# First layer of a graph network: 18 scatters and 8 dense tiles, then 17 and 9, in place of 18 and 8 in both halves of a loop body

## The reference, cut to what matters

```python
def scatter_mean(src, index, dim_size):
    s = jax.ops.segment_sum(src, index, num_segments=dim_size)
    cnt = jax.ops.segment_sum(jnp.ones((src.shape[0],), src.dtype), index, num_segments=dim_size)
    return s / jnp.maximum(cnt, 1.0)[:, None]

edge_attr_agg = scatter_mean(edge_attr, edge_index[0], x.shape[0])
combined = jnp.concatenate([x, edge_attr_agg], axis=1)
h = jax.nn.relu(combined @ W1 + b1)
return h @ W2 + b2
```

## Time and profile before

| | |
|---|---|
| median of 3 runs | 7578.14 us (7569.88 to 7579.32) |
| the profiled execution | 7575.93 us |
| its span, first to last instruction | 7574.1 us |
| VectorE busy, share of the span | 6223.6 us, 82% |
| GpSimd busy, share of the span | 5347.8 us, 71% |
| granted TensorE clock, mean | 0.835 |

### The profile page before, as it was taken

One profiled execution on the slowest core, in us unless ns is written; L12 is line 12 of the kernel. 1 busy time (PEld: TensorE's weight loads), 2 busy tenths in 40 slices (PEclk: granted clock), 3 DMA queues, 4 the chain that ended last, 5 costly groups with the idle time before them and its releaser, 6 DMA issues. The chain is left out here.

```text
span 7574.1 us, 145887 instructions
## 1 busy us (share of the span) xinstructions
PE 6258.4 (83%) x38830; PEld 4411.6 (58%) x38831; DVE 6223.6 (82%) x16834; ACT 4861.8 (64%) x11241; POOL 5347.8 (71%) x4893
## 2 busy tenths in 40 slices
PE   6988888888867999975777777777777999999995
PEld 3545545544546888865666666666674544444443
DVE  7999999999969999957999999999986555555554
ACT  5777778778737888844555555555524677777773
POOL 4888888888865566657777777777513777777776
PEclk9999999999978999965666666666655999999997
DMA  5444444444431111124343444444331222222222
GB/s 130 75 75 72 69 75 72 69 75 72 66 74 39 24 24 24 24 53 63 64 65 64 64 65 64 65 64 65 55 93 47 65 76 70 70 70 76 70 70 55
DMA packets 626461, 487.11 MB, mean 64 GB/s; under 512 B 513289, under 2 KB 530030, under 8 KB 616344
## 3 DMA queue, kind: packets, MB, share of 16 engines
q0 software_dynamic: 281600, 185.95, 21.1%
q1 hardware_dynamic: 342455, 293.43, 13.3%
q10 hardware_dynamic: 2304, 6.55, 0.3%
HBM read 303.43 MB, written 182.13 MB: 64 GB/s over the span
## 5 line engine op out<-in xcount | busy, mean ns | idle before, releaser
L977 POOL DMA_INDIRECT acc<-val,idx x1116 | 1722.6, 1544 | 379.5 <-issue 320.4
L1601 POOL DMA_INDIRECT tile_rows<-att_row_table,src_by_tile x1620 | 1531.0, 945 | 502.9 <-issue 490.9
L748 PE MATMUL banks<-part 128*128 128x490 bf16 (+1 forms) x7440 | 1569.5, 366 | 218.8 <-DVE part L831 218.8
L3032 POOL DMA_INDIRECT rows_l<-relation_table,idx x1302 | 1245.7, 957 | 430.6 <-issue 386.4
L3237 PE MATMUL banks<-h_parts,dense_onehot 128*128 128x448 bf16 x6510 | 1316.2, 359 | 102.2 <-ACT dense_onehot L2985 99.7
L2270 PE MATMUL banks<-tile_rows,prob 128*128 x4032 | 854.1, 380 | 539.8 <-DVE kept_l L2368 538.7
L748 PEld LDWEIGHTS banks<-part 128*128 128x128 bf16 x7440 | 694.3, 97 | 996.7 <-DVE part L831 280.9
L2270 PEld LDWEIGHTS banks<-tile_rows,prob 128*128 128x128 f32 x4032 | 769.0, 285 | 638.0 <-issue 637.9
L3237 PEld LDWEIGHTS banks<-h_parts,dense_onehot 128*128 128x128 bf16 x6510 | 620.5, 99 | 730.0 <-issue 178.7
L907 ACT ACTIVATE digit_distance<-iota_row,dst_digits_negated 128x128 bf16<-128x128 f32 (+1 forms) x3224 | 868.7, 357 | 2.1 <-ACT dst_digits_negated L896 0.2
L1296 POOL DMA_INDIRECT gathered_rows<-h_table,gathered_index x600 | 579.4, 966 | 397.3 <-DMA gathered_rows<-h_table,gathered_index 245.7
(11 more groups left out here) (449 smaller groups left out, 11835.1 us busy)
## 6 DMA issues: line engine op xcount, KB each, us to landing
src_rows<-src_by_column SPq DMA_DIRECT2D x63, 1152.0 KB, 5.9
piece_sums<-kept_l SPq DMA_DIRECT2D x252, 264.0 KB
running_sums<-run SPq DMA_DIRECT2D x62, 832.0 KB, 4.1
attr<-in_edge_attr SPq DMA_DIRECT2D x61, 624.0 KB
tile_rows<-att_row_table,src_by_tile POOLq DMA_INDIRECT x1620
rows_l<-relation_table,idx POOLq DMA_INDIRECT x1302
dense_code_rows<-src_by_column SPq DMA_DIRECT2D x62, 320.0 KB
acc<-val,idx POOLq DMA_INDIRECT x1116
```

Source lines behind the costliest of these rows:

```text
L748: last = e.matmul(ps[a][:, 0:ZW[a]], place0[(h * NZ + m) % 2][:, a, :], spread0[(h * NZ + m) % 2][n].rearrange("p b f -> p (b f)")[:, 0:ZW ...
L977: e.indirect_dma_start(acc_d[k], bass.IndirectOffsetOnAxis(ap=idx[h][:, r:r + 1], axis=0), val[h][:, r, :], None, compute_op=ALU.add).then ...
L1601: e.indirect_dma_start(to, None, hx_d, bass.IndirectOffsetOnAxis(ap=src_col[:, t:t + 1], axis=0))\
L3032: e.indirect_dma_start(g[h][:, r, :], None, y3_d, bass.IndirectOffsetOnAxis(ap=idx[h][:, r:r + 1], axis=0))\
```

## The change

In the second half of a loop body one tile goes dense instead of by scatter: 17 scatters in groups of 4, 4, 4, 4 and 1, and 9 dense tiles (spreads 4 to 8 one behind the other). The first half keeps 18 and 8. HS and NZ become pairs. The tile counters of dense tiles run over 17 tiles a loop (`z_count`). As 17 is odd, the buffer of a dense tile is now its number in its half, modulo 2: the last tile of a second half (m = 8) and the first one of the next first half (m = 0) then take the same buffer, and that first spread waits for one `z_add` more. The accumulator of a scatter is its number in the loop body, modulo 4; with 35 scatters in a loop the first three of the next one follow the last one into the same accumulator after three steps instead of four. Ahead of the loop, two of VectorE's instructions that split source numbers into digits become two each, and the scratch for the digits shares the room of `place0`.

```diff
-HS = 18
-NZ = HALF - HS
+HS = (18, 17)
+NZ = (HALF - HS[0], HALF - HS[1])
+NZL = NZ[0] + NZ[1]
+NSL = HS[0] + HS[1]
...
-        GROUPS = [(r, min(r + 4, HS)) for r in range(0, HS, 4)]
+        GROUPS = [[(r, min(r + 4, HS[h])) for r in range(0, HS[h], 4)] for h in range(2)]
+        ADDS = [len(range(k, NSL, NACC)) for k in range(NACC)]
...
+            hots0 = borrow(0, ZA * P)
+            place0 = [hots0.bitcast(bf16)[:, k * ZA * P:(k + 1) * ZA * P].rearrange("p (a c) -> p a c", c=P) for k in range(2)]
...
+            def z_count(i, h):
+                return i * NZL + h * NZ[0]
...
                             def z_add(m):
-                                e.wait_ge(s_spread, hh * NZ + m + 2)
+                                e.wait_ge(s_spread, z_count(i, h) + m + 2)
...
-                            for m in range(NG - 1, NZ):
+                            for m in range(NG - 1, NZ[h]):
                                 z_add(m)
...
-                    e.tensor_scalar(dig_i, src_z, 21400.0, None, ALU.mult).then_inc(s_digits, 1)
+                    e.tensor_scalar(of_half(dig_i, 0), src_z[0], 21400.0, None, ALU.mult)
+                    e.tensor_scalar(of_half(dig_i, 1), src_z[1], 21400.0, None, ALU.mult).then_inc(s_digits, 1)
...
                     def rest_one(hh, h):
...
-                        e.tensor_tensor(left0[0], pack[h][:, HS:HALF, :], high0[0], ALU.subtract).then_inc(s_left, 1)
+                        e.tensor_tensor(left0[0][:, 0:NZ[h], :], pack[h][:, HS[h]:HALF, :], high0[0][:, 0:NZ[h], :],
+                                        ALU.subtract).then_inc(s_left, 1)
...
                     def spread(hh, h, m):
...
-                        e.wait_ge(s_z, hh * NZ + m + 1)
-                        b = (h * NZ + m) % 2
+                        e.wait_ge(s_z, z_count(i, h) + m + (2 if m == 0 and h == 0 else 1))
+                        b = m % 2
...
-                            for k, (lo, hi) in enumerate(GROUPS):
+                            for k, (lo, hi) in enumerate(GROUPS[h]):
...
-                            for m in range(NG - 1, NZ):
+                            for m in range(NG - 1, NZ[h]):
                                 spread(hh, h, m)
...
-                            for r in range(HS):
-                                q, k = divmod(h * HS + r, NACC)
-
-                                e.wait_ge(s_add[k], (i * (2 * HS // NACC) + q) * 16 + 16)
+                            for r in range(HS[h]):
+                                q, k = divmod(h * HS[0] + r, NACC)
+
+                                e.wait_ge(s_add[k], (i * ADDS[k] + q) * 16 + 16)
```

## The result

The changed kernel takes 7659.49 us (median of 5 runs, 7657.05 to 7663.82) against 7572.81 us for the kernel before, measured beside it: a ratio of 1.0113, 95% interval 1.0098 to 1.0128. It is slower, by 87 us. The profiled execution took 7663.82 us, 87.9 us more than that of before. The prediction said 7654 us. All ratios in this document leave out the one execution that took far longer than the others, 18358 us, in the run of the kernel before with short target rows.

A forecast was written before the change was run, and what follows sets the result against it. The prediction took GpSimd (66.50 us a loop) to bound the kernel, VectorE with TensorE close behind: 65.56 + 2.78 + 0.58 = 68.92 us a loop, ending 78 us later. 7575.93 + 78 = 7654 us, range 7595 to 7680 us.

The forecast's parts named there:

- Two cycles: Late loop before the change: GpSimd's 66.50 us sets the pace, VectorE with TensorE needs 65.56 us, a slack of 0.94 us.
- The rule on occupancy: Highest occupancy marks the bottleneck: VectorE, 62.3 of 66.5 us, so the change would cost about 74 us; the prediction rejected it.
- The ninth tile: Spread 8, end of a second half: costs TensorE's step, 3.05 us a loop, bounds 2.65 to 3.05 us.
- The missing scatter tile: VectorE, second half: one compare of 0.27 us and 0.13 us of the `eq` compare saved, -0.40 us.
- The new wait: Spread 0 of a first half waits for `z_add` 8: 0.58 us on VectorE, bounds nothing to 3.05 us.
- Landings at three steps: GpSimd, first three scatters of a loop: taken as nothing, at most 4.6 us; slower rival 7700 us, chance 0.05.
- The base and what grew: VectorE's loop before the change, 65.56 us; `rest_one` and `rest_two` grow by 0.07 us each, 0.13 us for both.
- The sum: VectorE's loop becomes 68.92 us, last spread ends at 2206.8 us, whole kernel 7654 us; chance 0.73.
- The little-change rival: VectorE's loop: waits shrink, 67.12 us a loop, 7599 us, chance 0.11; within 15 us of no change, 0.04.

## Why the prediction was right, point by point

*Two cycles.* GpSimd was the pace of the kernel before: the shorter target rows gained nothing there, and its scatters fell behind the target rows until ACT's wait held the rest. VectorE with TensorE stood 1 us behind it: taking 7.4 us from GpSimd gained 1.1 us a body (65.4 for 66.5). That the slack was 0.94 us and not VectorE's 4.2 us of idle time decided the sign, and it was read off the first halves, in which GpSimd wasn't yet behind.

*The rule on occupancy* (the Trainium skill, page "Perfetto Trace Analysis", section "Identifying the Most-Contended Engine"). It named VectorE, by 94%, as what bounds the kernel before. The run with short target rows there (0.9996) contradicts it; in the changed kernel, where VectorE is busy 64.6 of 68.8 us, the same edit is worth 39 us of loop.

*The ninth tile* cost TensorE's step, 3.05 us (1030.60 to 1033.65), as taken; removing its wait gave back 0.33 us a body.

*The missing scatter tile* saves 0.48 us by the run with 18 and 9, not 0.40. A compare of 128 columns for `eq` takes 0.29 us in the changed kernel, as the slope gave; the other 0.08 us lies in and around the target rows.

*The new wait* measured 0.62 us of idle time for a forecast of 0.58, and in the kernel before it cost nothing, since it lay within the slack.

*Landings at three steps* were taken as nothing, and the run with 14 scatters shows that they were. Their upper bound of 4.6 us was far off: exposed, they reached 1.5 us at the longest and 1.8 us a body (57.0 / 31), of which 0.9 us is more than issue. The 1.3 us a loop of landing waits that the prediction adds beside them stands in no row: 26.2 us in 31 bodies are 0.85, and 65 x 0.3 us of them would be issue anyway.

*The base and what grew.* The 65.56 us read from the first six halves were 0.23 too long (65.33 with 14 scatters). `rest_one` and `rest_two` grew by 0.05 us each (0.62 for 0.57, 0.61 for 0.56), 0.10 for 0.13. And the target rows take 1.95 us a body in the changed kernel against 1.73 with 14 scatters in the kernel before (means); the sum has no term for these 0.22 us (next section). Put together, 65.33 + 3.05 - 0.48 + 0.10 + 0.62 + 0.22 = 68.84 us, which is what the trace shows. The base and the missing term cancel, and that is luck.

*The sum:* a body of 68.83 us against 68.92, and a start at 103.05 instead of 103.63 us, make the loop some 3.5 us shorter than forecast (30 x 0.09, 0.58 at the start, 0.22 in the first second half), which would have ended it at 2203.3 instead of 2206.8 us. It ended at 2213.4. The 10 us between are TensorE's clock, which the prediction took for constant (next section). The last spread thus came 6.6 us later than forecast, of a change of 85, because 3.5 us too much in the loop stood against 10 us left out; that the forecast came so near is in part luck.

*The little-change rival.* The loop that would end within 15 us of no change is 65.8 to 66.8 us by the prediction's own sum, not 66.3 to 66.9; the measured 68.8 is far from either.

## What the runs showed of the hardware that was not expected

Thirty of the 31 first halves follow a second one, and six of these take 34.9 instead of 33.3 us. One of them runs from 1380.58 to 1415.50 us. TensorE in order of time, then three stretches with the granted clock (third number from the right), then VectorE:

```profile
1386.71 4.91 PE L761 MATMUL banks<-part 128*128 128x490 bf16 x15 [1.32 <-DVE part L848]
```

```profile
1376.00:1386.00 10.00, 9.39 (x73) 5.28 (x71) 9.02 (x22) 2.33 (x8) 8.47 (x6) 1.00 0.47 75
1386.00:1389.00 3.00, 2.29 (x7) 0.92 (x8) 3.00 (x13) 2.97 (x11) 2.39 (x3) 0.67 0.20 11
1389.00:1392.00 3.00, 3.00 (x16) 1.62 (x14) 3.00 (x13) 0.78 (x2) 2.69 (x2) 0.76 0.40 22
```

```profile
1397.39 0.35 DVE L866 SCALAR_TENSOR_TENSOR scratch<-banks,src_tile,strict_lower 128x128 f32<-128x128 f32 x1 [2.10 <-ACT banks L936]
```

TensorE was idle for 1.32 us ahead of `z_add` 0, and the granted clock then lay at 0.67 and 0.76 of full speed on the mean of two stretches of 3 us, so for part of them at its lower level of 1.2 GHz. Over the 4.91 us of this `z_add` the mean was 0.65, and 3.2 / 0.65 is 4.9, so the clock accounts for its whole length; behind it, from 1391.62 us, it was 1.00 again. The sums of group 1 came late behind it, ACT's `val` and rows too, and VectorE waited 2.10 us ahead of group 3 in place of 0.41. Six such halves at 1.62 us are 9.7 us. All thirty have the idle time of 1.3 us, because spread 0 starts late while TensorE is through with the sums and counts; in the kernel before it is 0.75 us. Behind the first half, the long `z_add` 0 was found only in the five kernels with the longer wait, each time behind 1.3 us of idle: 6 of 30 in the changed kernel, 9, 4 and 2 in its versions with 14 scatters, with short target rows and with 18 and 9, and 3 in the kernel before with the wait alone. In the eight kernels without it, where TensorE is idle for 0.9 us at most ahead of `z_add` 0, there is none. So in these kernels it came only behind 1.3 us of idle time, and most times that idle time passed without it. The six of the changed kernel stand 208 us apart, which is three bodies, with one gap of 621 us, nine bodies; why those and not the others was not tried.

A second thing holds for two of the four instructions of the target rows, the first (L879) and the third (L884), which take 0.18 and 0.23 us as a rule, and now and then up to 0.53. GpSimd and VectorE in order of time, in a second half of the changed kernel:

```profile
1020.33 1.54 POOL L994 DMA_INDIRECT acc<-val,idx  x1 [0.30 <-issue]
1020.94 0.42 DVE L884 TENSOR_SCALAR target_f<-target_f,dump_row 128x17 f32<-128x17 f32 x1
```

The long instruction starts 0.61 us behind the start of a scatter and ends 1.03 us behind it. In the thirteen traces 307 of these two instructions (in the short form, of the one that is like the first) took more than 0.27 us; 295 of them started 0.50 to 0.75 us behind the start of a scatter, and each of the 295 ended 1.02 to 1.04 us behind it, whether it took 0.28 or 0.53 us; the other 12 ended 1.5 us behind it. So nearly every long one started in the same part of a scatter and lasted until 1.03 us into it. How often that happens differs from kernel to kernel, as GpSimd's row lies against VectorE's: 31 times in the changed kernel, 10 in the kernel before, 47 in the run with 17 scatters, 3 in the run with 14. That is the 0.22 us a body that the prediction's sum has no term for, and the 0.21 us between the runs with 17 and 14 scatters. No run changed this alone, and what in the scatter holds VectorE is not shown.

## What to carry to other kernels

Before work is moved from the engine that sets the pace to another, read the second cycle's own length from a stretch in which the first engine isn't yet behind; idle time overstates the slack, since much of it is waiting inside the second cycle, which stays. Where buffers are handed back, two things tell that an engine sets the pace: the other engines wait for it again and again, and its own work falls further behind from half to half until their waits hold the distance; an unbroken row alone doesn't. Here one scatter (1.85 us) went for a tile that cost 2.8 us and a wait of 0.6 us in a cycle with 0.94 us to spare. The move pays once the second cycle is shortened along with it: with three buffers, another order and fewer small instructions, the same 17 and 9 run 0.5% faster than the kernel before. These three were tried together; the third buffer and the short target rows were also tried alone, and neither was enough. Without the move the body could not go below GpSimd's 36 x 1.847 = 66.5 us, as the short target rows in the kernel before showed.
